# Load and store pieces of the full regions in a two-convolution kernel: 1, 4, 4, 3, 1 and 3, 3, 4, 3 tiles in place of 1, 3, 3, 3, 2, 1 and 2, 3, 3, 3, 2

## The chip, the core and the metric

One core of a Trainium2 chip runs the whole program. The metric is device microseconds of one execution; a change is read against the median of the runs before. Engines are named as the profile names them: PE (TensorE matmul), PEld (its weight loads), DVE (VectorE), ACT (ScalarE), POOL (GpSimd), SP (SyncE, which here only issues transfers). SPq and ACTq are the transfer queues of SP and ACT.

## The reference

Input x has 16 heads of 1024 x 1024 float32 (64 MB); the output has the same shape. Two layers follow each other:

```
y   = x + bias(t, s, head)            # bias: a small ReLU network of log distance, lower triangle
out = y (w + 1) + (y qw1) qw2 + (y kw1) kw2 + y qdd + y kdd
```

The first layer adds to each head a bias that depends on row t and column s only through their distance and a scale per row. The second mixes the 16 heads at every (t, s): a part of the 16 x 16 mixing matrix depends on the row t (w, qw1, qw2, qdd), a part on the column s (kw1, kw2, kdd).

## The kernel before, in words

**Tiles.** The 1024 columns are cut into 8 blocks of 128, so that 16 heads x 8 blocks fill 128 partitions. A tile is 8 rows (8 x 128 = 1024 floats a partition, 512 KB in all), and there are 128 tiles. They go in 11 regions (`REGION_TILES`, L22): region 0 has 6 tiles, regions 1 to 9 have 13 (the full ones), region 10 has 5.

**Homes.** SBUF holds three homes of 13 tile slots. Region k has home k mod 3: its x is loaded one slot further on than its y, y is written over it, and the mixed result goes to the home of region k+2. So x of region k+2 can land in a slot only when the result of region k that lies there has been stored. The last tile of x of a region lies in slot 0 of the next home, where the first result tile of the region before last lies.

**Steps.** PE takes each region in 16 column steps (`b_columns`, L763 to L774) and then one row step for each tile (`a_rows`, L750 to L761). ACT and DVE take the results of the column steps to the home in turn (L528, L641), and DVE adds those of a row step to them (`finish_tile`, L643 to L651); after that the tile can be stored. Between these steps lies the bias of the tiles of the next region: POOL makes the hidden layer (L462), ACT its ReLU (L501), PE multiplies it by the small weights (`bias_tile`, L776 to L792), and DVE (L671, L677) and ACT (L512) add the bias to x. Tile 0 of the next region has its turn at column step 4, tile 1 at step 5, then about one tile for every two steps; tile 12 comes at row step 11 (`bias_step`, L184). From tile 64 on (region 4) there are two hidden tiles for each tile in place of one.

**Row matrices.** The 16 x 16 matrices of the row steps lie in DRAM (a_mats) in chunks of 4 tiles. SP loads a chunk into one of two buffers (`load_mats_a`, L328 to L334, 4 transfers), and POOL spreads it (L439) for PE, four tiles ahead of the row step. POOL does this in line with the hidden tiles, so a chunk that comes late holds up the hidden tiles too.

**Transfers.** A load piece is 8 transfers, one for each block (`load_x`, L315 to L326), all on SP. A store piece is 8 transfers too: 4 on SP (`store_upper`, L336 to L340) and 4 on ACT, in two portions of 2 at the two row steps after the piece's last tile (`portions_at`, L282, and L542 to L547). A load waits for the stores that free its slots, by one semaphore for each store piece (`out_done`).

**The order on SP** is written out by hand (L382 to L406): for region k and its row steps T = 0 to 12, SP first issues the chunk of row matrices that falls due there (every fourth tile, so the T differs from region to region: 0, 4, 8, 12 in regions 1, 5 and 9; 3, 7, 11 in 2 and 6; 2, 6, 10 in 3 and 7; 1, 5, 9 in 4 and 8), then at T = 6 the last piece of x of region k+1, then the store piece whose last tile is T (the last store piece a step early in the list), then at T = 7, 10 and 12 (`AHEAD`) the pieces 0, 1 and 2 of x of region k+2. The pieces that are left (3 and 4) come first in the list of region k+1. Each of these waits in line: a store piece waits until DVE has finished its last tile, and all that stands behind it on SP waits with it.

In what follows S0, S1, ... are the store pieces of the region, X0, X1, ... the load pieces of region k+2, XL the last load piece of region k+1, and M with a number the chunk that falls due at that row step. The list between the first store and X2 is then, for a region 1 as an example:

```
before: M0 S0(T1) M4 S1(T4) XL(T6) S2(T7) X0(T7) M8 S3(T10) X1(T10) S4(T11) M12 X2(T12)
after:  M0 S0(T2) M4 S1(T5) XL(T6) X0(T7) M8 S2(T9) X1(T10) S3(T11) M12 X2(T12)
```

Of the kernel before, what the change touches and what calls it, by code (L numbers as in the profile page):

```python
# [21 lines left out]
REGION_TILES = (6,) + (13,) * 9 + (5,)  # L22
REGIONS = len(REGION_TILES)
# [2 lines left out]
HALF_TILES = ALL_TILES // 2  # L26
HOME_TILES = max(REGION_TILES)
HOMES = 3
STORE_PIECES = {6: (2, 2, 2), 13: (2, 3, 3, 3, 2), 5: (2, 1, 1, 1)}
STORE_SEMS = max(len(sizes) for sizes in STORE_PIECES.values())  # L30
LOAD_PIECES = {6: (1, 2, 3), 13: (1, 3, 3, 3, 2, 1), 5: (1, 4)}
AHEAD = (7, 10, 12)
PORTIONS = (2, 2)
CHUNK = 32
# [25 lines left out]
def build(nc, x, W1, b1, W2, b2, c, L_mult, init_L, qw1, qw2, kw1, kw2, qdd, kdd, w, out):  # L60
# [6 lines left out]
    with ExitStack() as ctx:  # L67
# [84 lines left out]
        def tile_of(k, T):  # L152
            return FIRST_TILE[k] + T
# [19 lines left out]
        def a_tile(k, T):  # L173
            return SETUP_TILES + FIRST_TILE[k] + COL_TILES * (k + 1) + T
# [5 lines left out]
        def emptied(i):  # L180

            return main_taken[i % 2], i // 2 + 1
# [32 lines left out]
        def piece_start(sizes, i):  # L215
            return sum(sizes[:i])

        def times(pieces, i, k):

            return sum(i < len(pieces(r)) for r in range(k + 1))  # L220

        def store_pieces(k):
            return STORE_PIECES[REGION_TILES[k]]

        def load_pieces(k):
            return LOAD_PIECES[REGION_TILES[k]]

        def piece_of(sizes, T):
            return min(i for i in range(len(sizes)) if T < sum(sizes[:i + 1]))
# [13 lines left out]
        def x_slot(k, T):  # L243
            return (y_slot(k, T) + 1) % (HOMES * HOME_TILES)
# [25 lines left out]
        def home_rows(b, slot, n):  # L270
            return of_block(homes, HOMES * HOME_TILES * COLS, b, slot * COLS, [[W, n], [1, W]])

        def store_block(eng, k, i, b):
            T, n = piece_start(store_pieces(k), i), store_pieces(k)[i] * ROWS
            t0 = tile_of(k, T) * ROWS
            return eng.dma_start(out[0, :, t0:t0 + n, b * W:(b + 1) * W], home_rows(b, mixed_slot(k, T), n))  # L276
# [29 lines left out]
        @block.sync  # L306
        def _(sp):
            def load_compact(part, v1, v2, vd):
                for dst, src in ((first[part], v1), (second[part], v2)):
                    sp.dma_start(dst.rearrange("p (b i) -> p b i", b=BLOCKS),  # L310
                                 src.rearrange("o (b p) g i m -> p (o b) (g i m)", p=P)).then_inc(weights_in[part], DMA)
                sp.dma_start(diag[part].rearrange("p (b m) -> p b m", b=BLOCKS),
                             vd.rearrange("o (b p) g m -> p (o b) (g m)", p=P)).then_inc(weights_in[part], DMA)

            def load_x(k, i):  # L315
                T, n = piece_start(load_pieces(k), i), load_pieces(k)[i]
                if k >= 1 and T + 1 >= HOME_TILES:

                    sp.wait_ge(out_done[0], times(store_pieces, 0, k - 1) * PER_PIECE)
                elif k >= 2 and T + 1 < REGION_TILES[k - 2]:  # L320
                    left = piece_of(store_pieces(k - 2), min(T + n, REGION_TILES[k - 2] - 1))
                    sp.wait_ge(out_done[left], times(store_pieces, left, k - 2) * PER_PIECE)
                t0 = tile_of(k, T) * ROWS
                for b in BLOCK_ORDER:
                    sp.dma_start(home_rows(b, x_slot(k, T), n * ROWS),
                                 x[0, :, t0:t0 + n * ROWS, b * W:(b + 1) * W]).then_inc(x_in[i], DMA)  # L326

            def load_mats_a(v):  # L328
                if v >= A_RING:
                    sp.wait_ge(unit_ready, (v - A_RING + 1) * (CHUNK // UNIT))  # L330
                for g in range(GROUPS):
                    src = bass.AP(a_mats.tensor, v * H * H * CHUNK, [[H * CHUNK, H], [0, GS], [1, H * CHUNK]])
                    sp.dma_start(mats_in[GP * g:GP * (g + 1), v % A_RING * H * CHUNK:(v % A_RING + 1) * H * CHUNK], src)\
                        .then_inc(a_in[v % A_RING], DMA)  # L334

            def store_upper(k, i):  # L336
                taken, count = emptied(a_tile(k, piece_start(store_pieces(k), i + 1) - 1))
                sp.wait_ge(taken, count)
                for b in BLOCK_ORDER[sum(PORTIONS):]:
                    store_block(sp, k, i, b).then_inc(out_done[i], DMA)  # L340

            def load_mats_b():
                for b in range(BLOCKS):
                    sp.dma_start(of_block(mats_b, RGP * W, b, (b // GS % WIDE * GP + b % GS) * W, [[GS * W, H], [1, W]]),
                                 b_mats[b]).then_inc(b_in, DMA)

            def save_mats(part):
                for half in range(2):
                    taken, count = emptied(turned_tile(part, half))
                    sp.wait_ge(taken, count)  # L350
                    src = turned[part][:, half * COLS:(half + 1) * COLS]
                    m = slice(half * (H // 2), (half + 1) * (H // 2))
                    if part == "b":
                        dst = b_mats[:, m].rearrange("b m n j -> (m n) b j")
                        src = src.rearrange("p (b j) -> p b j", b=BLOCKS)
                    else:
                        dst = a_mats[:, m].rearrange("v m n e -> (m n) v e")
                        src = src.rearrange("p (v e) -> p v e", e=CHUNK)
                    sp.dma_start(dst, src).then_inc(mats_out[part], DMA)

            load_compact("b", kw1, kw2, kdd)
            load_x(0, 0)
            load_compact("a", qw1, qw2, qdd)
            sp.dma_start(w_eye, w.rearrange("g m n -> g (m n)").partition_broadcast(P)).then_inc(weights_in["a"], DMA)
            load_x(0, 1)
            load_x(0, 2)
            save_mats("b")
            sp.wait_ge(mats_out["b"], 2 * DMA)
            sp.wait_ge(mats_zeroed, 1)
            load_mats_b()  # L370
            for i in range(3):
                load_x(1, i)
            save_mats("a")
            load_x(1, 3)
            sp.wait_ge(mats_out["a"], 2 * DMA)
            for v in range(A_RING):
                load_mats_a(v)
            load_x(1, 4)
            sp.wait_ge(tables_made, 3)
            sp.dma_start(late_scales, scale_late).then_inc(scales_out, DMA)  # L380
            loaded = [3, 5] + [0] * (REGIONS - 2)
            for k in range(REGIONS):  # L382

                while k + 1 < REGIONS and loaded[k + 1] < min(5, len(load_pieces(k + 1))):
                    load_x(k + 1, loaded[k + 1])
                    loaded[k + 1] += 1
                if k == 3:
                    sp.wait_ge(scales_out, DMA)
                    sp.wait_ge(nd_ready, PART // 2 // ROWS)
                    sp.dma_start(row_scale[:, 0:PART // 2], late_scales[:, 0:PART // 2]).then_inc(scales_in, DMA)  # L390
                if k == 5:
                    sp.wait_ge(nd_ready, PART // ROWS)
                    sp.dma_start(row_scale[:, PART // 2:], late_scales[:, PART // 2:]).then_inc(scales_in, DMA)
                for T in range(REGION_TILES[k]):
                    v = chunk_behind(tile_of(k, T))
                    if v is not None:
                        load_mats_a(v)
                    if k + 1 < REGIONS and len(load_pieces(k + 1)) > 5 and T == min(6, REGION_TILES[k] - 4):
                        load_x(k + 1, 5)
                    for i in range(len(store_pieces(k))):  # L400
                        if T == piece_start(store_pieces(k), i + 1) - 1 - (i == 4 and k < REGIONS - 1):
                            store_upper(k, i)
                    if k + 2 < REGIONS and (T in AHEAD or k == 0 and T == REGION_TILES[0] - 1) \
                            and loaded[k + 2] < len(load_pieces(k + 2)):
                        load_x(k + 2, loaded[k + 2])
                        loaded[k + 2] += 1  # L406
            for i in range(len(out_done)):
                sp.wait_ge(out_done[i], times(store_pieces, i, REGIONS - 1) * PER_PIECE)
# [429 lines left out]
```

## Time and profile before

| what | value |
|---|---|
| median of 3 runs | 895.82 us |
| lowest and highest run | 891.65 and 903.48 us |
| the profiled execution | 896.75 us |
| its span in the trace | 894.9 us |
| mean granted TensorE clock | 0.894 of full |
| PE, DVE, ACT, POOL busy | 78%, 54%, 44%, 57% of the span |
| read from and written to HBM | 77.61 MB and 69.47 MB |

The span runs from the first to the last instruction of the trace; 1.85 us of the profiled execution lie around it. A busy share is a mean over stages with different limits: in the first half of the tiles POOL has one hidden tile for each tile, in the second half two.

### The profile page before, as it was taken

How to read it: one execution, taken by the hardware profiler on the slowest of the kernel's cores; microseconds unless marked ns; L12 is line 12 of the kernel's file. 1: busy time of each engine (PE TensorE's matmuls, PEld its weight loads, DVE VectorE, ACT ScalarE, POOL GpSimd, SP SyncE). 2: the span in 40 equal slices, each digit the busy share in tenths (PEclk: the TensorE clock that was granted, in tenths of full speed). 3: DMA queues.
4: the chain of work that ended last, by engine and by line, in shares of the span. 5: the costliest groups of instructions: out<-in, count | busy, mean ns of one | idle time of the engine just before them, and what ended most of it. 6: DMA issues, size and time to landing. Idle time of an engine off the chain costs nothing. (4 is left out here: it accounts for less than half of the span.)

```text
span 894.9 us, 28881 instructions
## 1 busy us (share of the span) xinstructions
PE 699.0 (78%) x12836; PEld 586.1 (65%) x12836; DVE 481.0 (54%) x629; ACT 395.8 (44%) x428; POOL 513.4 (57%) x463
## 2 busy tenths in 40 slices
PE   0466767986998798696699859969988896699764
PEld 0254566875887688585577657756866685589664
DVE  7667625863693595475346625653475365335412
ACT  5756536544743663563245325433543453232000
POOL 4524823734475257368558937985898588635300
PEclk9876978988998899899899979998999999799857
DMA  6578559597778979877885888589859897843905
GB/s 129 137 169 147 132 145 205 128 227 169 181 185 208 208 149 223 213 159 150 189 195 125 201 185 188 113 185 215 183 123 184 180 198 151 212 111 73 258 7 118
DMA packets 302936, 148.98 MB, mean 166 GB/s; under 512 B 31964, under 2 KB 298588, under 8 KB 302812
## 3 DMA queue, kind: packets, MB, share of 16 engines
q1 hardware_dynamic: 232928, 113.56, 57.5%
q10 hardware_dynamic: 69884, 33.58, 16.3%
q8 instruction: 101, 1.65, 0.8%
q14 instruction: 23, 0.19, 0.1%
HBM read 77.61 MB, written 69.47 MB: 164 GB/s over the span
## 5 line engine op out<-in xcount | busy, mean ns | idle before, releaser
L462 POOL TENSOR_TENSOR hidden<-log_table,row_scale 128x1024 f32<-128x1024 f32 x192 | 364.3, 1913 | 218.3 <-PE bias L789 210.4
L772 PEld LDWEIGHTS main<-homes,mats_b 64*64 64x64 f32 (+1 forms) x6656 | 316.9, 189 | 150.3 <-ACT homes L528 65.1
L772 PE MATMUL main<-homes,mats_b 64*64 64x104 f32 (+2 forms) x6656 | 332.5, 274 | 106.1 <-ACT homes L528 50.7
L501 ACT ACTIVATE hidden<-hidden,b_col 128x1024 f32<-128x1024 f32 x192 | 221.0, 1152 | 259.6 <-POOL hidden L462 187.6
L759 PEld LDWEIGHTS main<-homes,mats_a 64*64 64x64 f32 x4096 | 239.2, 136 | 51.3 <-issue 37.4
L759 PE MATMUL main<-homes,mats_a 64*64 64x128 f32 x4096 | 256.0, 279 | 5.2 <-POOL mats_a L439 3.5
L439 POOL TENSOR_TENSOR mats_a<-mats_in,own_block 128x256 f32<-128x256 f32 x256 | 153.6, 655 | 143.0 <-DMA mats_in<-a_mats 112.9
L651 DVE TENSOR_TENSOR homes<-main,homes 128x1024 f32<-128x1024 f32 x128 | 156.7, 1225 | 59.4 <-PE main L759 54.3
L641 DVE COPY homes<-main 128x832 f32<-128x832 f32 (+1 forms) x80 | 77.7, 971 | 192.1 <-PE main L772 189.2
L789 PE MATMUL bias<-hidden,w_blocks 64*32 64x256 f32 (+1 forms) x2048 | 120.4, 528 | 58.0 <-ACT hidden L501 46.4
L677 DVE SCALAR_TENSOR_TENSOR homes<-bias,b_col,homes 64x256 f32<-64x256 f32 x256 | 122.9, 480 | 76.7 <-DMA homes<-in_x 52.8
L528 ACT ACTIVATE homes<-main 128x832 f32<-128x832 f32 (+2 forms) x96 | 73.4, 764 | 141.2 <-PE main L772 125.9
L671 DVE SCALAR_TENSOR_TENSOR homes<-bias,b_col,homes 128x512 f32<-128x512 f32 x128 | 90.3, 747 | 68.0 <-PE bias L789 58.2
L512 ACT ACTIVATE homes<-homes,b_col 64x512 f32<-64x512 f32 x128 | 89.9, 754 | 63.5 <-DMA homes<-in_x 52.3
L789 PEld LDWEIGHTS bias<-hidden,w_blocks 64*32 64x32 f32 x2048 | 24.8, 108 | 79.4 <-issue 60.2
L298 DVE TENSOR_TENSOR homes<-homes 128x2048 f32<-128x2048 f32 x4 | 12.3, 3123 | 0.1
L719 PE MATMUL bias<-relu_b,w_blocks 64*32 64x1 f32 x4 | 0.3, 191 | 13.7 <-DVE w_blocks L626 13.7
L719 PEld LDWEIGHTS bias<-relu_b,w_blocks 64*32 64x32 f32 x4 | 0.2, 136 | 13.6 <-issue 13.6
L495 ACT ACTIVATE mats_b<-zero_col 128x8192 f32<-128x8192 f32 x1 | 7.0, 7012 | 0.0
L712 PE MATMUL main<-homes 128*128 128x128 f32 x32 | 5.6, 350 | 0.6 <-DVE homes L606 0.6
L712 PEld LDWEIGHTS main<-homes 128*128 128x128 f32 x32 | 5.0, 183 | 1.5 <-issue 0.8
L601 DVE TENSOR_TENSOR homes<-homes 128x2048 f32<-128x2048 f32 x2 | 4.6, 2292 | 0.1
(40 smaller groups left out, 33.0 us busy)
## 6 DMA issues: line engine op xcount, KB each, us to landing
homes<-in_x SPq DMA_DIRECT2D x224, 192.0 KB, 6.2
out_mixed<-homes SPq DMA_DIRECT2D x108, 192.0 KB, 4.8
out_mixed<-homes ACTq DMA_DIRECT2D x108, 192.0 KB, 5.4
out_mixed<-homes SPq DMA_DIRECT2D x88, 128.0 KB, 3.5
out_mixed<-homes ACTq DMA_DIRECT2D x88, 128.0 KB, 3.6
homes<-in_x SPq DMA_DIRECT2D x160, 64.0 KB, 4.4
homes<-in_x SPq DMA_DIRECT2D x80, 128.0 KB, 4.5
mats_in<-a_mats SPq DMA_DIRECT2D x128, 64.0 KB
```

Of the source, the lines that this page charges most:

```text
L439: spread_half = nc.gpsimd.tensor_tensor(bass.AP(mats_a, w % A_RING_UNITS * A_UNIT + q * GP, [[A_RING_UNITS * A_UNIT, P], [GS, H], [1, GS], ...
L462: nc.gpsimd.tensor_tensor(hidden_tile(u, g).rearrange("p (j b s) -> p j b s", b=2, s=W), bass.AP(log_table, t0 - SLOTS * W * g, [[2 * TABL ...
L501: nc.scalar.activation(hidden_tile(u, g), hidden_tile(u, g), ACT.Relu, bias=b1_col[:, 0:1])\
L512: add = nc.scalar.activation(y_rows(high_half, k, T, b), x_rows(high_half, k, T, b), ACT.Identity, bias=b2_col[high_half, 1:2])
L528: nc.scalar.activation(mixed_columns(k, C), column_sums(k, C), ACT.Copy)\
L641: dve.tensor_copy(mixed_columns(k, C), column_sums(k, C)).then_inc(main_taken[b_tile(k, C) % 2], 1)
L651: dve.tensor_tensor(at, main[:, i % 2, :], at, ALU.add).then_inc(main_taken[i % 2], 1)
L671: add = dve.scalar_tensor_tensor(out=y_rows(whole, k, T, b), in0=falling(u, b), scalar=b2_col[:, 0:1], in1=x_rows(whole, k, T, b), op0=ALU ...
L677: add = dve.scalar_tensor_tensor(out=y_rows(low_half, k, T, b)[:, some], in0=falling_part(u, part, b), scalar=b2_col[low_half, 0:1], in1=x ...
L759: mm = pe.matmul(main[of_wide(g), i % 2, j * W:(j + 1) * W], a_weights(g, w, j), y_row(k, T, g, j), start=True, stop=True)
L772: mm = pe.matmul(main[at, i % 2, j * W:j * W + REGION_TILES[k] * ROWS], b_weights(at, C * ROWS + j), y_column(k, at, C * ROWS + j), start= ...
L789: mm = pe.matmul(bias[quadrant(q), u % 2, b * BANK:b * BANK + n * W], w2_blocks[of, :], rows[:, b, part * n:(part + 1) * n, :], start=True ...
```

## The change

Full regions are loaded in pieces of 1, 4, 4, 3 and 1 tiles and stored in pieces of 3, 3, 4 and 3. That is 8 load transfers and 8 store transfers (4 on SP, 4 on ACT) fewer for each of the nine full regions, with the same bytes. The four load pieces before the last are again followed by `AHEAD` and by the head of the next region's list, which now holds one piece (3) in place of two. Regions 0 and 10 keep their pieces.

```diff
--- before.py
+++ after.py
@@ -26,9 +26,9 @@
 HALF_TILES = ALL_TILES // 2
 HOME_TILES = max(REGION_TILES)
 HOMES = 3
-STORE_PIECES = {6: (2, 2, 2), 13: (2, 3, 3, 3, 2), 5: (2, 1, 1, 1)}
+STORE_PIECES = {6: (2, 2, 2), 13: (3, 3, 4, 3), 5: (2, 1, 1, 1)}
 STORE_SEMS = max(len(sizes) for sizes in STORE_PIECES.values())
-LOAD_PIECES = {6: (1, 2, 3), 13: (1, 3, 3, 3, 2, 1), 5: (1, 4)}
+LOAD_PIECES = {6: (1, 2, 3), 13: (1, 4, 4, 3, 1), 5: (1, 4)}
 AHEAD = (7, 10, 12)
 PORTIONS = (2, 2)
 CHUNK = 32
@@ -222,6 +222,10 @@
         def store_pieces(k):
             return STORE_PIECES[REGION_TILES[k]]
 
+        def loads_ahead(k):
+
+            return len(load_pieces(k)) - (REGION_TILES[k] == HOME_TILES)
+
         def load_pieces(k):
             return LOAD_PIECES[REGION_TILES[k]]
 
@@ -375,13 +379,14 @@
             sp.wait_ge(mats_out["a"], 2 * DMA)
             for v in range(A_RING):
                 load_mats_a(v)
-            load_x(1, 4)
+            for i in range(4, loads_ahead(1)):
+                load_x(1, i)
             sp.wait_ge(tables_made, 3)
             sp.dma_start(late_scales, scale_late).then_inc(scales_out, DMA)
-            loaded = [3, 5] + [0] * (REGIONS - 2)
+            loaded = [loads_ahead(0), loads_ahead(1)] + [0] * (REGIONS - 2)
             for k in range(REGIONS):
 
-                while k + 1 < REGIONS and loaded[k + 1] < min(5, len(load_pieces(k + 1))):
+                while k + 1 < REGIONS and loaded[k + 1] < loads_ahead(k + 1):
                     load_x(k + 1, loaded[k + 1])
                     loaded[k + 1] += 1
                 if k == 3:
@@ -395,13 +400,13 @@
                     v = chunk_behind(tile_of(k, T))
                     if v is not None:
                         load_mats_a(v)
-                    if k + 1 < REGIONS and len(load_pieces(k + 1)) > 5 and T == min(6, REGION_TILES[k] - 4):
-                        load_x(k + 1, 5)
+                    if k + 1 < REGIONS and REGION_TILES[k + 1] == HOME_TILES and T == min(6, REGION_TILES[k] - 4):
+                        load_x(k + 1, loads_ahead(k + 1))
                     for i in range(len(store_pieces(k))):
-                        if T == piece_start(store_pieces(k), i + 1) - 1 - (i == 4 and k < REGIONS - 1):
+                        if T == piece_start(store_pieces(k), i + 1) - 1 - (REGION_TILES[k] == HOME_TILES and i == len(store_pieces(k)) - 1 and k < REGIONS - 1):
                             store_upper(k, i)
                     if k + 2 < REGIONS and (T in AHEAD or k == 0 and T == REGION_TILES[0] - 1) \
-                            and loaded[k + 2] < len(load_pieces(k + 2)):
+                            and loaded[k + 2] < loads_ahead(k + 2):
                         load_x(k + 2, loaded[k + 2])
                         loaded[k + 2] += 1
             for i in range(len(out_done)):
```

## Rows read from the trace of the kernel before

**Rows 1.** Busy time of each engine, share of the span, instructions (the page).

```profile
PE 699.0 (78%) x12836; PEld 586.1 (65%) x12836; DVE 481.0 (54%) x629; ACT 395.8 (44%) x428; POOL 513.4 (57%) x463
```

**Rows 2.** List of waits: who waited for what, us in total, times, longest.

```profile
POOL mats_a L439 <- DMA mats_in<-a_mats: 112.9, 17, 17.6
...
DVE homes L677 <- DMA homes<-in_x: 52.8, 9, 9.7
ACT homes L512 <- DMA homes<-in_x: 52.3, 10, 12.0
```

**Rows 3.** Timeline of PE: start, us, instruction, count [idle before, releaser].

```profile
221.69 5.81 PE L772 MATMUL main<-homes,mats_b 64*64 64x104 f32 x64 [8.28 <-ACT homes L528]
...
445.92 6.72 PE L772 MATMUL main<-homes,mats_b 64*64 64x104 f32 x96 [7.95 <-ACT homes L528]
```

**Rows 4.** Timeline of SP's queue, row steps of region 1, S0 to X1.

```profile
168.09 3.41 SPq L276 DMA_DIRECT2D out_mixed<-homes  x4
171.55 3.33 SPq L333 DMA_DIRECT2D mats_in<-a_mats  x4
175.59 4.41 SPq L276 DMA_DIRECT2D out_mixed<-homes  x4
180.04 8.23 SPq L325 DMA_DIRECT2D homes<-in_x  x8
188.32 4.42 SPq L276 DMA_DIRECT2D out_mixed<-homes  x4
192.78 6.29 SPq L325 DMA_DIRECT2D homes<-in_x  x8
199.12 3.19 SPq L333 DMA_DIRECT2D mats_in<-a_mats  x4
202.35 2.69 SPq L276 DMA_DIRECT2D out_mixed<-homes  x4
205.09 9.69 SPq L325 DMA_DIRECT2D homes<-in_x  x8
```

**Rows 5.** Timeline of DVE, bias of tile 1 in region 2.

```profile
219.38 1.97 DVE L677 SCALAR_TENSOR_TENSOR homes<-bias,b_col,homes 64x256 f32<-64x256 f32 x4 [9.65 <-DMA homes<-in_x]
```

**Rows 6.** Busy time by stretch, S0 to X1's landing; last three: granted clock, DMA share, GB/s.

```profile
168.00:219.40 51.40, 41.61 (x728) 36.80 (x724) 29.64 (x44) 18.96 (x23) 29.82 (x32) 0.91 0.88 193
```

**Rows 7.** Timeline of DVE: tiles 2 to 5 of region 2, tiles 4 and 5 of region 4.

```profile
248.03 2.46 DVE L651 TENSOR_TENSOR homes<-main,homes 128x1024 f32<-128x1024 f32 x2
...
252.40 2.46 DVE L651 TENSOR_TENSOR homes<-main,homes 128x1024 f32<-128x1024 f32 x2
...
405.92 1.23 DVE L651 TENSOR_TENSOR homes<-main,homes 128x1024 f32<-128x1024 f32 x1 [0.38 <-PE main L759]
407.73 1.23 DVE L651 TENSOR_TENSOR homes<-main,homes 128x1024 f32<-128x1024 f32 x1 [0.59 <-PE main L759]
```

**Rows 8.** Timeline of SP's queue: X1 of region 7, S2 and X1 of region 8.

```profile
697.04 8.14 SPq L325 DMA_DIRECT2D homes<-in_x  x8
...
758.36 2.67 SPq L276 DMA_DIRECT2D out_mixed<-homes  x4
...
775.10 9.16 SPq L325 DMA_DIRECT2D homes<-in_x  x8
```

**Rows 9.** Timeline of SP's queue: M5 and M9 of region 4.

```profile
411.94 2.67 SPq L333 DMA_DIRECT2D mats_in<-a_mats  x4
...
432.79 3.41 SPq L333 DMA_DIRECT2D mats_in<-a_mats  x4
```

**Rows 10.** Timeline of POOL: spreading after a wait, regions 4, 6 and 9.

```profile
440.63 1.19 POOL L439 TENSOR_TENSOR mats_a<-mats_in,own_block 128x256 f32<-128x256 f32 x2 [8.48 <-DMA mats_in<-a_mats]
...
600.11 1.20 POOL L439 TENSOR_TENSOR mats_a<-mats_in,own_block 128x256 f32<-128x256 f32 x2 [3.75 <-DMA mats_in<-a_mats]
...
831.21 4.65 POOL L439 TENSOR_TENSOR mats_a<-mats_in,own_block 128x256 f32<-128x256 f32 x8 [4.14 <-DMA mats_in<-a_mats]
```

**Rows 11.** Issues by size: times, KB each, median us to landing (the page).

```profile
homes<-in_x SPq DMA_DIRECT2D x224, 192.0 KB, 6.2
...
homes<-in_x SPq DMA_DIRECT2D x8, 256.0 KB, 7.5
```

## The prediction

> **What bounds the kernel now.** I began with the busy times. PE, the busiest engine, works 78% of the span [rows 1], so some 196 us of it are gaps, and the question is who makes them. The list of waits names two late transfers: row matrices, for which POOL waited 112.9 us in 17 waits, and x, for which DVE and ACT waited 52.8 and 52.3 us, mostly side by side [rows 2]. PE's timeline shows where this is paid. Early in the column steps of nearly every region PE stands still: 8.28 us in region 2, 7.95 us in region 5 [rows 3]. The releaser is ACT each time, but ACT was itself held. In region 2, ACT and DVE waited for x of tile 1, which came at 219.38 after a wait of 9.65 us [rows 5]. In region 5, POOL had waited 8.48 us, up to 440.63, for a chunk of row matrices [rows 10], and ACT's next ReLU stood in line before the copy that PE needed.
>
> Both transfers come from SP's list, so I read SP's queue next. In region 1 it issues without a break from 175.59 to 214.78 [rows 4], while the DMA engines are 88% busy at 193 GB/s [rows 6]. The list begins when DVE finishes the first tiles and ends with X1, issued from 205.09; so PE's gap moves by exactly as much as X1, or the late M, moves against the start of the row steps. The rest of a region is PE's own work or POOL's, which the change leaves alone. So I work out for each region how far the transfer that ends its gap moves.
>
> **The change part by part.** It has four terms.
>
> a) S1 waits for tile 5 in place of tile 4. In the first half DVE finishes the pair in 2.46 us, so 1.23 us later; in the second half 407.73 - 405.92 = 1.8 us later [rows 7]. S0 also waits a tile longer (tile 2), and in regions 1 and 2 a chunk stands between S0 and S1. In region 2 tile 2 is done at 248.03 + 1.23 = 249.3; S0 and M take 3.41 + 3.33 = 6.7 us [rows 4], so S1 starts at 256.0, 2.4 us behind the end of tile 4 at 253.6. I take +2.4 in regions 1 and 2. In region 3 the chunk (T = 2) is now issued ahead of S0, which leaves +1.2. In the second half row steps come more slowly and the chunk fits between the two: +1.8.
>
> b) S2 moves from T = 7 to T = 9 and so behind X0, and behind a chunk due at T = 8 or 9. For these SP's line is shorter by one S2: 4.42 us in region 1 [rows 4], 2.67 us in region 8 [rows 8], the first and the last of eight, whose mean is 3.5: -3.5.
>
> c) Ahead of X1 there now stand S0, S1, S2 with 10 tiles, where S0 to S3 with 11 stood. One S of four tiles takes the place of an S3 of three, which took 2.69 us [rows 4]. By bytes four tiles take 4/3 of it, by issues the same: 0 to +0.9. I take +0.9, since a load of 64 KB transfers took 6.29 us and one of 192 KB 9.69 us [rows 4]: size counts.
>
> d) X1 has 4 tiles in place of 3. Region 8 shows eight 256 KB issues in 9.16 us (x of region 10 has such a piece); seven with 192 KB took 9.69 us (first) to 8.14 us (last), mean 8.1 [rows 4, 8]: +1.1. By the median landing times it is 7.5 - 6.2 = +1.3 [rows 11], by bytes alone 0.52 MB at 193 GB/s = +2.7 [rows 6]; the least is -0.5, the first against the 256 KB row. The row with the size itself is nearest.
>
> Fewer issues: 8 loads and 4 stores fewer on SP cost nothing ahead of X1 beyond (b) and (c), the rest lie behind X1, where SP catches up. ACT loses 4 issues a region, beside waits of its own: 0, at the most -2.6 us a region in ACT time, covered by its wait for PE or POOL. What is late next is X2, four tiles from tile 5, wanted eight column steps after tile 1, some 8 x 2.2 = 17.5 us (half of 252.40 - 248.03 for a step [rows 7]). It is issued behind S3 (at most 4.0) and a chunk (2.7) and takes 9.2: 15.9 us behind X1, a slack of 1.6 us. At 193 GB/s X2 alone takes 10.9 us and the slack is gone: 0 to +0.1 here, up to 2 us a region if S3 or M is slow. I take 0.
>
> XL is issued by (a) later. It ends the row steps of regions 1 and 2 with a PE gap, but X1 ends a gap behind it, so that is covered. In the second half XL needs S0's ACT half, issued two row steps later; up to +1 us in regions 4 to 8, 0 taken.
>
> **The sum.** Regions whose gap ends with X1: region 0 issues x of region 2 in a run, so (d) alone, +1.1. Regions 1 and 2: 2.4 - 3.5 + 0.9 + 1.1 = +0.9 each. Region 3: -0.3. Region 7, with 1.8 for (a): +0.3. Together +2.9.
>
> Regions whose gap ends with a chunk. In 4 and 8 the chunk at T = 5 now stands ahead of S1's wait, where it was issued at 411.94 behind it; that shortens the line to M9 by its 2.67 us [rows 9], and S2 is gone from it too (2.7 to 2.8 us in both): 1.8 - 2.7 - 2.7 = -3.6 each. The earlier wait for M5 vanishes, but POOL then only reaches M9 sooner, so its gain isn't added. Region 5 (M8): 1.8 - 3.5 = -1.7. Region 6 waits for M7, up to 600.11 [rows 10]; it stands behind S1 and XL but was ahead of S2 already: +1.8. Region 9 waits for M4, up to 831.21 [rows 10], behind S0, which opens a tile later: +1.8. Together -3.6 x 2 - 1.7 + 1.8 + 1.8 = -5.3.
>
> 2.9 - 5.3 = -2.4 us. Against the profiled execution, 896.75 us (span 894.9), that is 894.4; the median, 0.93 us lower, gives 893.4. I forecast 893.5 us: no difference that can be told, since about 2% (18 us) is what a measurement here tells from none.
>
> **The rivals.** *Faster: SP's issuing is the bound, not the bytes.* Then (c) and (d) are 0, and (a) is covered because SP is behind anyway. For it: between M4's end (174.88) and S1 (175.59) SP waited only 0.7 us, then not at all up to X1 [rows 4]. Regions 1, 2, 3, 5 and 7 gain 3.5 each, 4 and 8 2.7 + 2.7 each: -17.5 - 10.8 = -28, 868 us. Against it: the DMA share of 0.88, and the 192 KB pieces that take longer to issue than the 64 KB ones. The Trainium skill (DMA: Bandwidth & Descriptors, section Rules for kernel authors) says many small transfers should be coalesced into a large one; it speaks for this rival. The trace agrees only in part: 256 KB lands in 7.5 us against 6.2, less than by its bytes [rows 11].
>
> *Slower: the DMA engines are the bound from S0 to X1's landing.* Up to that landing 18 tiles' worth must pass: S0 to S3 (11), S4's ACT half (1), XL, X0 and X1 (5), two chunks (1). After it is S0 to S2 (10), S3's ACT half (1.5), 6 tiles of x, the chunks: 18.5. S2 behind X0 then gains X1 nothing. The half tile is 0.26 MB at 193 GB/s = 1.4 us, the later start is (a), and X1's extra tile comes last of all, with none of its transfers complete before: 2.7 by bytes. That is 2.4 + 1.4 + 2.7 = 6.5 in regions 1 and 2, 5.3 in 3, 5.9 in 7, 2.7 in 0; 6 and 9 pay 1.8 each; 4, 5 and 8 lose their gain. Sum +31, 927 us; it decides when X1 lands over 53 us behind the old S0 in region 1. Against it: 12% of that stretch is idle, 6 us, enough to take the half tile; with the extra tile at 1.1 and no half tile it is half, some 910 us. The Trainium skill (DMA: Bandwidth & Descriptors, section Issuing engines are not separate DMA queues) says that transfers of SP and ACT run on the same 16 DMA engines, which is why ACT's halves count here. The trace agrees as far as SP's issues stretch to 1 us apiece at 180.04 while ACT stores [rows 4].
>
> **How the numbers follow.** The forecast has 0.60, the faster rival 0.22, the slower 0.18. Half of the faster one's price is 882, which is still within 2%; below 877.9 (faster by over 2%) I put 0.16, above 913.7 (slower) 0.12, within 0.72. The range leaves a tenth on each side: the faster one's 870 at the one end, a little over the slower one's half price, 914, at the other. The forecast's own range, from the bounds of c, d and the 1 us of XL, is 884 to 905.
>
> **What would show it.** In SP's queue of region 1 after the change: S1 some 2 us later against the row steps, X0 and M8 about 1 us earlier, S2 directly ahead of X1, X1 some 9 to 10 us long and landing within 2 us of before (51.3 us behind the old S0). The total of POOL's waits for row matrices should fall by 5 to 15 us, with the waits for M5 in regions 4 and 8 gone and that in region 6 longer; DVE's and ACT's waits for x should stay within 10 us. I am wrong if X1 lands over 3 us earlier or later in most regions, or if DVE waits at tile 5, for X2.

## The result and the profile after

The changed kernel takes 927.34 us (median of 4 runs, 925.97 to 928.00), the kernel before 893.74 us beside it (891.29 to 903.48): a ratio of 1.0347 with an interval of 1.0295 to 1.0399. By the medians it is slower by 33.6 us; 893.5 was forecast, and the range ended at 914. The profiled execution took 927.26 us (span 925.4). Here and below a ratio leaves out executions in a slower state (one of four in run 10, two of ten in run 11), and a median does not.

The page's busy line after the change, to be read beside [rows 1]. The engines do the same work, only the span is longer, so the time came as gaps.

```profile
PE 698.4 (75%) x12836; PEld 584.7 (63%) x12836; DVE 479.6 (52%) x629; ACT 395.6 (43%) x428; POOL 513.3 (55%) x463
```

The list of waits after, for [rows 2] (line, what was waited for, us in total, times, longest). The waits for row matrices rose by 5 us, those of ACT for x from 52.3 to 78.2, those of DVE from 52.8 to 73.3. The second DVE line for x, L676, works in the second half of the tiles and had 9.8 us in two waits before. Of its five waits now, four are for tile 1: 5.64, 2.74 and 2.95 us in the column steps of regions 5, 6 and 7, where nothing was waited for before, and 12.85 us in those of region 8, where it was 8.63.

```profile
POOL mats_a L444 <- DMA mats_in<-a_mats: 118.3, 17, 16.2
ACT homes L517 <- DMA homes<-in_x: 78.2, 10, 12.3
...
DVE homes L682 <- DMA homes<-in_x: 73.3, 10, 11.8
...
DVE homes L676 <- DMA homes<-in_x: 24.8, 5, 12.8
```

PE's timeline after, at the places of [rows 3] (start, us, what, in brackets the idle time ahead and its end): the gap early in region 2's column steps is now 10.46 us, where it was 8.28. The one in region 5 fell a little, from 7.95 to 7.56 us.

```profile
236.94 5.81 PE L777 MATMUL main<-homes,mats_b 64*64 64x104 f32 x64 [10.46 <-ACT homes L533]
...
468.74 6.52 PE L777 MATMUL main<-homes,mats_b 64*64 64x104 f32 x96 [7.56 <-ACT homes L533]
```

SP's queue in region 1 after, for [rows 4]: S0, M4, S1, then XL and X0 in one row of 16 issues, M8, S2, X1.

```profile
180.56 4.39 SPq L280 DMA_DIRECT2D out_mixed<-homes  x4
184.99 4.81 SPq L337 DMA_DIRECT2D mats_in<-a_mats  x4
189.85 3.66 SPq L280 DMA_DIRECT2D out_mixed<-homes  x4
193.55 14.49 SPq L329 DMA_DIRECT2D homes<-in_x  x16
208.08 2.51 SPq L337 DMA_DIRECT2D mats_in<-a_mats  x4
210.63 6.08 SPq L280 DMA_DIRECT2D out_mixed<-homes  x4
216.75 11.11 SPq L329 DMA_DIRECT2D homes<-in_x  x8
```

DVE's timeline after, the first instruction on tile 1 and the first on tile 5, for [rows 5]: tile 1 came at 234.62, tile 5 was hardly waited for.

```profile
234.62 1.97 DVE L682 SCALAR_TENSOR_TENSOR homes<-bias,b_col,homes 64x256 f32<-64x256 f32 x4 [11.84 <-DMA homes<-in_x]
...
253.14 1.98 DVE L682 SCALAR_TENSOR_TENSOR homes<-bias,b_col,homes 64x256 f32<-64x256 f32 x4 [0.63 <-DMA homes<-in_x]
```

The stretch after that answers to [rows 6] (stretch and us, busy of PE, PEld, DVE, ACT and POOL, granted clock, DMA share, GB/s). It begins 1.6 us ahead of S0; from S0 on the DMA share is 0.85 and the rate 191 GB/s, where 0.88 and 193 stood. On average the DMA engines are not fuller than before.

```profile
179.00:234.60 55.60, 39.41 (x700) 34.53 (x694) 28.00 (x39) 18.89 (x22) 28.06 (x31) 0.89 0.83 185
```

**Measured from the start of region 1's row steps** (162.95 before, 172.28 after), in us:

| | S0 | S1 | XL | M8 | X1 issued from | to | tile 1 landed |
|---|---|---|---|---|---|---|---|
| before | 5.1 | 12.6 | 17.1 | 36.2 | 42.1 | 51.8 | 56.4 |
| after | 8.3 | 17.6 | 21.3 | 35.8 | 44.5 | 55.6 | 62.3 |

S1 opens 4.9 us later. With S2 gone from behind XL, M8 is level again. S2 at 6.08 us in place of S3's 2.69 then sets X1 back by 2.3. X1 itself adds 3.6, of which 1.4 in issuing and 2.2 between its last issue and its landing (4.6 before, 6.8 after).

The same reading for all the regions whose late issue of X1 was forecast to end a gap, in us against the kernel before (the region is that of the row steps in which X1 is issued; the landing is the last of its eight):

| region | 1 | 2 | 3 | 7 |
|---|---|---|---|---|
| forecast | +0.9 | +0.9 | -0.3 | +0.3 |
| X1 landed | +5.9 | +4.9 | +5.8 | +3.8 |
| of it: X1 begun | +2.3 | +0.4 | +2.9 | +0.8 |
| X1's eight issues | +1.4 | +4.1 | +2.3 | +2.4 |
| from its last issue to its landing | +2.2 | +0.4 | +0.6 | +0.6 |

So X1 itself costs 2.9 to 4.5 us more, 3.5 in the mean, and outside region 1 most of it lies in issuing. X1 of region 2, before and after:

```profile
283.53 6.53 SPq L325 DMA_DIRECT2D homes<-in_x  x8
```
```profile
299.27 10.63 SPq L329 DMA_DIRECT2D homes<-in_x  x8
```

**Where the time arises**, from PE's timeline: by how much the first row step or column step of a region starts later than before (the two profiled executions lie 30.5 us apart). The largest single steps are region 1's beginning, then 5.7 to 6.6 from one region's row steps to the next in regions 1 to 4, and 6.7 in the column steps of region 8. Two stretches give 4.5 back each: rows of 4 to columns of 5, and rows of 8 to columns of 9.

| region | 1 | 2 | 3 | 4 | 5 | 6 | 7 | 8 | 9 | 10 |
|---|---|---|---|---|---|---|---|---|---|---|
| column steps | +6.3 | +13.6 | +18.1 | +24.7 | +23.2 | +22.6 | +28.4 | +25.7 | +27.9 | +29.8 |
| row steps | +9.3 | +15.3 | +21.1 | +27.7 | +22.6 | +26.2 | +27.2 | +32.4 | +27.4 | +30.5 |

Set against the prediction's sum (a region's share runs from its row steps to those of the next, region 0's from region 1's column steps): 6.3 us at region 1's beginning, for which it has no term; 26.6 in regions 0, 1, 2, 3 and 7 together, put at +2.9; and -2.4 in regions 4, 5, 6, 8 and 9, put at -5.3.

The 6.3 us at region 1 come before any store of a full region. At the start SP issues three pieces of region 1's x, then writes the row matrices to DRAM (`a_mats`), issues a fourth piece, and only then loads the first chunks of row matrices. SP's queue and POOL there, before: the three pieces are seven tiles.

```profile
43.75 20.01 SPq L325 DMA_DIRECT2D homes<-in_x  x24
63.80 7.82 SPq L359 DMA_DIRECT2D a_mats<-homes  x2
...
80.51 7.81 SPq L333 DMA_DIRECT2D mats_in<-a_mats  x8
```
```profile
87.33 4.75 POOL L439 TENSOR_TENSOR mats_a<-mats_in,own_block 128x256 f32<-128x256 f32 x8 [6.96 <-DMA mats_in<-a_mats]
```

And after: the three pieces are nine tiles, 26.65 us in place of 20.01, and POOL starts on the row matrices 5.35 us later. Its hidden tiles stand behind them, and PE's second row step of region 0 begins at 102.41, where it was 97.09.

```profile
43.22 26.65 SPq L329 DMA_DIRECT2D homes<-in_x  x24
69.91 7.39 SPq L363 DMA_DIRECT2D a_mats<-homes  x2
...
86.76 6.68 SPq L337 DMA_DIRECT2D mats_in<-a_mats  x8
```
```profile
92.68 4.62 POOL L444 TENSOR_TENSOR mats_a<-mats_in,own_block 128x256 f32<-128x256 f32 x8 [8.35 <-DMA mats_in<-a_mats]
```

### The profile page after: what moved, and what is told of

Read it like the earlier page. It is cut to its first block and busy times, and to the rows that moved or that the text cites. A ratio compares the mean times of both kernels' runs of the same rounds, so it can differ in the third digit from the quotient of the medians.

```text
span 925.4 us, 28737 instructions
## 1 busy us (share of the span) xinstructions
PE 698.4 (75%) x12836; PEld 584.7 (63%) x12836; DVE 479.6 (52%) x629; ACT 395.6 (43%) x428; POOL 513.3 (55%) x463
## 5 line engine op out<-in xcount | busy, mean ns | idle before, releaser
L777 PE MATMUL main<-homes,mats_b 64*64 64x104 f32 (+2 forms) x6656 | 331.9, 274 | 123.7 <-ACT homes L533 62.2
L764 PEld LDWEIGHTS main<-homes,mats_a 64*64 64x64 f32 x4096 | 236.3, 134 | 55.8 <-issue 40.5
L764 PE MATMUL main<-homes,mats_a 64*64 64x128 f32 x4096 | 253.4, 278 | 10.3 <-POOL mats_a L444 9.4
L682 DVE SCALAR_TENSOR_TENSOR homes<-bias,b_col,homes 64x256 f32<-64x256 f32 x256 | 122.9, 480 | 100.6 <-DMA homes<-in_x 73.3
L676 DVE SCALAR_TENSOR_TENSOR homes<-bias,b_col,homes 128x512 f32<-128x512 f32 x128 | 90.3, 747 | 75.1 <-PE bias L794 50.4
L517 ACT ACTIVATE homes<-homes,b_col 64x512 f32<-64x512 f32 x128 | 89.7, 753 | 87.2 <-DMA homes<-in_x 78.2
L302 DVE TENSOR_TENSOR homes<-homes 128x2048 f32<-128x2048 f32 x4 | 12.3, 3122 | 0.1
L525 ACT ACTIVATE homes<-main 128x1024 f32<-128x1024 f32 x4 | 4.0, 1023 | 2.0 <-PE main L717 2.0
```

What stands on the lines that cost most here:

```text
L517: add = nc.scalar.activation(y_rows(high_half, k, T, b), x_rows(high_half, k, T, b), ACT.Identity, bias=b2_col[high_half, 1:2])
L676: add = dve.scalar_tensor_tensor(out=y_rows(whole, k, T, b), in0=falling(u, b), scalar=b2_col[:, 0:1], in1=x_rows(whole, k, T, b), op0=ALU ...
L682: add = dve.scalar_tensor_tensor(out=y_rows(low_half, k, T, b)[:, some], in0=falling_part(u, part, b), scalar=b2_col[low_half, 0:1], in1=x ...
L764: mm = pe.matmul(main[of_wide(g), i % 2, j * W:(j + 1) * W], a_weights(g, w, j), y_row(k, T, g, j), start=True, stop=True)
L777: mm = pe.matmul(main[at, i % 2, j * W:j * W + REGION_TILES[k] * ROWS], b_weights(at, C * ROWS + j), y_column(k, at, C * ROWS + j), start= ...
```

## The experiments

Ratios are against the kernel before, timed beside them on the same chip: 895.55 us for runs 1 to 4, 897.26 for 5 to 8, 894.58 for 9 to 12. In all of them but run 4 a load also waits for every store piece whose tiles it overwrites, not for the last one only; the changed kernel itself waits for the last one. No cost of it is seen: SP's waits for stores ahead of loads come to 5.6 us in the changed kernel, to none in run 1, and to 5.0 to 5.4 in runs 2, 3, 5, 6 and 9.

**1. The loads alone.**

```diff
-STORE_PIECES = {... 13: (3, 3, 4, 3) ...}
+STORE_PIECES = {... 13: (2, 3, 3, 3, 2) ...}
```

> The change's load pieces (1, 4, 4, 3, 1) with the old store pieces (2, 3, 3, 3, 2). Theory A (x of the first waited piece, X1, comes late because it is 4 tiles and the transfer engines are full): the gap in regions 1 to 3 grows by about 3.5 us each, the start by 6 us, x of region 2 by 3 us; some 910 to 916 us. Theory B (the later gates of the store pieces S0 and S1 are what costs): only the start and region 2 are paid, 900 to 905 us. Theory C (the four-tile store S2 ahead of X1 costs): as B.

928.26 us, ratio 1.0357 (1.0320 to 1.0395): above what any theory gave. All of the loss is there with the old stores. SP's queue of region 1 shows X1, and DVE's timeline its landing:

```profile
216.23 10.50 SPq L330 DMA_DIRECT2D homes<-in_x  x8
```
```profile
233.94 1.97 DVE L683 SCALAR_TENSOR_TENSOR homes<-bias,b_col,homes 64x256 f32<-64x256 f32 x4 [16.95 <-DMA homes<-in_x]
```

Tile 1 lands 7.2 us behind the last issue and 62.2 us behind the row steps' start (171.76 here), as late as in the changed kernel. The stores aren't needed for that.

**2. The stores alone.**

```diff
-LOAD_PIECES = {... 13: (1, 4, 4, 3, 1) ...}
+LOAD_PIECES = {... 13: (1, 3, 3, 3, 2, 1) ...}
```

> The change's store pieces (3, 3, 4, 3) with the old load pieces (1, 3, 3, 3, 2, 1). Theory A: X1 is three tiles again, so regions 1 to 3 lose 2 us each at most and some of it is given back in regions 4, 5 and 8: 893 to 902 us. Theory B: +5 us in each of regions 1 to 3 and about 2 us in 6 and 9: 908 to 915 us. Theory C: 2 to 3 us in each of regions 1 to 3: 898 to 905 us.

891.22 us, ratio 0.9937 (0.9906 to 0.9969), 4 us faster. From its X1's first issue (206.11) to tile 1 it takes 14.0 us, as before (219.38 - 205.09 = 14.3):

```profile
220.12 1.97 DVE L683 SCALAR_TENSOR_TENSOR homes<-bias,b_col,homes 64x256 f32<-64x256 f32 x4 [6.26 <-DMA homes<-in_x]
```

So the terms (a), (b), (c) and the gain at M9 together are a small gain, as forecast, and the later gates alone are not the loss. They are felt, though: X1 of region 1 begins 45.0 us behind the row steps' start, where it was 42.1.

**3. The changed kernel with region 1's x in the old pieces.**

```diff
-            return LOAD_PIECES[REGION_TILES[k]]
+            return (1, 3, 3, 3, 2, 1) if k == 1 else LOAD_PIECES[REGION_TILES[k]]
```

> The changed kernel, but x of region 1 alone is loaded in the old pieces (1, 3, 3, 3, 2, 1). In the trace of the changed kernel the first row matrices are issued 6 us later than before, behind 9 tiles of x in place of 7, and region 1 begins 6 us later. If that is a cost of its own, 921 us (6 less than the changed kernel's 927). If it is covered by a later wait, 926 to 928 us.

917.34 us, ratio 1.0213 (1.0167 to 1.0258). Lower than both values: the start, of which the prediction says nothing, is worth about 10 us, and some 22 are left.

**4. The kernel before with S0 and S1 held back by a tile.**

```diff
+        def held(k, i):
+            return int(REGION_TILES[k] == HOME_TILES and i < 2)
...
-                taken, count = emptied(a_tile(k, piece_start(store_pieces(k), i + 1) - 1))
+                taken, count = emptied(a_tile(k, piece_start(store_pieces(k), i + 1) - 1 + held(k, i)))
```

(The place in SP's list and ACT's portions move with it.)

> The kernel before with all its pieces, but the store pieces S0 and S1 of full regions are issued one tile later, on both queues. Theory B: X1 moves with S1, 4 to 5 us in each of regions 1 to 3, 2 us in 6, 7 and 9, less 3 us in 4 and 8: 903 to 910 us. Theory A and C: the line to X1 catches up by its own slack, under 2 us in each of regions 1 to 3: 892 to 900 us.

906.87 us, ratio 1.0109 (1.0063 to 1.0154). Term (a) is real, and about 10 us by itself; run 2 shows that the rest of the new store layout pays for it. In region 1, S1 begins 15.0 us behind the row steps' start, 2.4 later than before, which is the price that (a) has there.

**5. X1 of three tiles again, X2 of four.**

```diff
-LOAD_PIECES = {... 13: (1, 4, 4, 3, 1) ...}
+LOAD_PIECES = {... 13: (1, 3, 4, 4, 1) ...}
```

> The change's store pieces, and five load pieces as in the change, but of 1, 3, 4, 4 and 1 tiles: X1 has three tiles again, X2 and X3 have four. Theory A (X1's own size delays tile 1 of the next region): regions 1 to 3 go back to what the run with the store pieces alone has, the start keeps half of its loss (8 tiles ahead of the first row matrices, where 9 or 7 stood): 893 to 900 us. Theory D (fewer and larger pieces cost wherever they stand): 910 us or more.

909.78 us, ratio 1.0174 (1.0114 to 1.0234): 10 us above theory A's range and at the edge of D's, so neither is met. One tile less in X1 wins 1.7 points back, although the bytes of a region are the same. What stays is the start (region 1's column steps begin 6.3 us late here too) and X2, whose four tiles now begin at tile 4 and are waited for; in the column steps of region 3:

```profile
325.02 1.97 DVE L683 SCALAR_TENSOR_TENSOR homes<-bias,b_col,homes 64x256 f32<-64x256 f32 x4 [7.45 <-DMA homes<-in_x]
```

**6. X1's four tiles as 2 and 2, issued in a run.** Bytes, places and the start stay as in the changed kernel; only the first two tiles now have transfers and a semaphore of their own. (The start-up list is written so that the same nine tiles go first.)

```diff
-LOAD_PIECES = {... 13: (1, 4, 4, 3, 1) ...}
+LOAD_PIECES = {... 13: (1, 2, 2, 4, 3, 1) ...}
...
-                        load_x(k + 2, loaded[k + 2])
-                        loaded[k + 2] += 1
+                        for more in range(2 if T == 10 and REGION_TILES[k + 2] == HOME_TILES else 1):
+                            load_x(k + 2, loaded[k + 2])
+                            loaded[k + 2] += 1
```

> The changed kernel with X1's four tiles as two pieces of two, issued one right behind the other at the same place (1, 2, 2, 4, 3, 1); the same tiles of region 1 as in the changed kernel go ahead of the first row matrices. Bytes and order of all transfers stay, only tiles 1 and 2 are signalled when their half has landed. If what costs is that tile 1 waits for the whole piece, the gap shrinks by 4 to 6 us in regions 0 to 3 and 7: 902 to 912 us. If what costs are the bytes ahead of X1, nothing is gained: 922 to 930 us.

913.64 us, ratio 1.0179 (1.0122 to 1.0237), nearer to the side of the wait for a whole piece. SP's queue, and DVE on tile 1 and on tile 5:

```profile
209.33 13.61 SPq L330 DMA_DIRECT2D homes<-in_x  x16
```
```profile
222.00 1.97 DVE L682 SCALAR_TENSOR_TENSOR homes<-bias,b_col,homes 64x256 f32<-64x256 f32 x4 [4.79 <-DMA homes<-in_x]
...
249.01 1.97 DVE L682 SCALAR_TENSOR_TENSOR homes<-bias,b_col,homes 64x256 f32<-64x256 f32 x4 [10.18 <-DMA homes<-in_x]
```

All four tiles are issued from 209.33 to 222.94, longer than in the changed kernel, and yet tile 1 is taken 12.7 us behind the first issue (17.9 there). The other half lands 17.4 us behind the first issue, nearly as late as the whole piece does (17.9). The wait then passes to the four tiles behind, the changed kernel's X2: 10.18 us at tile 5, where the changed kernel showed 0.63.

**7. X1 ahead of S2.**

```diff
-AHEAD = (7, 10, 12)
+AHEAD = (7, 8, 12)
```

> The changed kernel with X1 issued at row step 8 in place of 10, ahead of the four-tile store S2. Theory C (S2 ahead of X1 costs): regions 1 to 3 gain S2's issue, 4 to 6 us each, and region 7 some: 905 to 915 us. If ACT's half of S2 and the transfer engines hold X1 back all the same: 920 to 928 us.

955.77 us, ratio 1.0682 (1.0635 to 1.0729): no theory had this. X1 does land sooner in region 1 (57.1 us behind the row steps' start, 62.3 in the changed kernel). But where a chunk falls due at T = 9 or 10, it now stands behind X1. In regions 3, 4, 7 and 8 POOL waits 18.1 to 23.1 us for it. SP's queue in region 7 (XL, X0 and X1 in one row, S2, M10), and POOL's wait for M10:

```profile
708.10 27.40 SPq L330 DMA_DIRECT2D homes<-in_x  x24
735.55 7.97 SPq L280 DMA_DIRECT2D out_mixed<-homes  x4
743.57 2.73 SPq L338 DMA_DIRECT2D mats_in<-a_mats  x4
```
```profile
749.77 1.19 POOL L445 TENSOR_TENSOR mats_a<-mats_in,own_block 128x256 f32<-128x256 f32 x2 [23.07 <-DMA mats_in<-a_mats]
```

POOL's waits for row matrices come to 155.7 us. The run tells nothing of X1's length; it shows what a chunk pays that stands behind a long piece.

**8. A short first piece, all of it short.** Pieces of 1, 2, 3, 3, 3 and 1, X1 (two tiles) and X2 issued together at T = 10 as in run 6; this also puts six tiles in place of nine ahead of the writing of the row matrices.

```diff
-LOAD_PIECES = {... 13: (1, 4, 4, 3, 1) ...}
+LOAD_PIECES = {... 13: (1, 2, 3, 3, 3, 1) ...}
```

> The change's store pieces with loads of 1, 2, 3, 3, 3 and 1 tiles, X1 and X2 issued one behind the other at row step 10; 6 tiles of region 1 ahead of the first row matrices. Theory A carried on: X1 lands 2 to 3 us sooner than with three tiles, the start gains 3 us: 878 to 888 us. If the wait only passes on to tile 3 (X2): 888 to 895 us, as with the store pieces alone.

886.77 us, ratio 0.9895 (0.9855 to 0.9934): faster than both kernels, than the one before by about 1%.

**9. The changed kernel with the old start, X1 and X2 as 2 and 2 each.** Region 1's pieces as in run 3; the rest:

```diff
-LOAD_PIECES = {... 13: (1, 4, 4, 3, 1) ...}
+LOAD_PIECES = {... 13: (1, 2, 2, 2, 2, 3, 1) ...}
...
+                        for more in range(2 if T in (10, 12) and REGION_TILES[k + 2] == HOME_TILES else 1):
```

> The changed kernel with x of region 1 in the old pieces and, in the later full regions, the two pieces of four tiles each cut into two of two, issued one right behind the other (1, 2, 2, 2, 2, 3, 1): bytes, order and places of the changed kernel, with finer signals and 16 more issues a region. If the loss is the start and the wait of a tile for the rest of its piece, all of it is gone: 886 to 896 us, as with the store pieces alone (891). If fewer issues or the bytes matter too: over 900 us.

883.98 us, ratio 0.9856 (0.9797 to 0.9914), better than expected. Against run 3, which has the same tiles in the same places of SP's list, only the halves are new, and the ratio falls from 1.0213 to 0.9856. SP's queue and DVE in region 1:

```profile
201.04 11.90 SPq L330 DMA_DIRECT2D homes<-in_x  x16
```
```profile
211.89 1.97 DVE L684 SCALAR_TENSOR_TENSOR homes<-bias,b_col,homes 64x256 f32<-64x256 f32 x4 [5.18 <-DMA homes<-in_x]
```

The four tiles take 11.90 us to issue (11.11 in one piece), but tile 1 is there 10.9 us behind the first issue, ahead of the end of the last. The second half lands at 15.9 us.

**10. Run 8's loads with the old stores.**

```diff
-STORE_PIECES = {... 13: (3, 3, 4, 3) ...}
+STORE_PIECES = {... 13: (2, 3, 3, 3, 2) ...}
```

> The loads of 1, 2, 3, 3, 3 and 1 tiles that gave 887 us, with the old store pieces (2, 3, 3, 3, 2). If the new store pieces are worth what they gave alone (0.6%): 889 to 895 us. If the later gates of S0 and S1 cost what they cost alone (1.1%): 876 to 884 us.

884.82 us, ratio 0.9853 (0.9767 to 0.9938). Beside run 8's 0.9895 (0.9855 to 0.9934) the two store layouts can't be told apart with such loads.

**11. The kernel before with region 1's x alone in the new pieces.**

```diff
-            return LOAD_PIECES[REGION_TILES[k]]
+            return (1, 4, 4, 3, 1) if k == 1 else LOAD_PIECES[REGION_TILES[k]]
```

> The kernel before, with x of region 1 alone in the change's pieces (1, 4, 4, 3, 1), 9 tiles in place of 7 ahead of the first row matrices. If the start is a cost of its own: 6 to 10 us over the kernel before, 901 to 907 us. If region 0 hides it: under 2 us more.

903.54 us, ratio 1.0088 (1.0043 to 1.0132): some 8 us by the ratio, from the start alone. Its SP queue shows 25.53 us for the nine tiles, and region 1's column steps begin 6.4 us late.

```profile
43.18 25.53 SPq L330 DMA_DIRECT2D homes<-in_x  x24
...
85.79 6.77 SPq L338 DMA_DIRECT2D mats_in<-a_mats  x8
```

**12. Run 8 with three tiles ahead of the writing of the row matrices and nine behind their load.**

```diff
-            for i in range(3):
+            for i in range(2):
                 load_x(1, i)
...
-            load_x(1, 3)
...
-            for i in range(4, loads_ahead(1)):
+            for i in range(2, loads_ahead(1)):
                 load_x(1, i)
```

> The run with loads of 1, 2, 3, 3, 3 and 1 tiles and the new store pieces (887 us), with 3 tiles of x of region 1 in place of 6 ahead of the first row matrices and the other 9 behind them. If those bytes set the start: 3 to 6 us less, 881 to 884 us. If x of region 1 then comes late itself: 887 us or more.

893.55 us, ratio 0.9980 (0.9950 to 1.0010), behind run 8's 0.9895. The x of region 1 is now what is late: DVE waited 15.30 us for it up to 83.15. Fewer tiles ahead of the row matrices help only until x itself is wanted.

```profile
83.15 1.97 DVE L683 SCALAR_TENSOR_TENSOR homes<-bias,b_col,homes 64x256 f32<-64x256 f32 x4 [15.30 <-DMA homes<-in_x]
```

## Why the prediction was wrong

**Term (d) was undersized by a factor of three.** It was put at +1.1, from how long the pieces take to issue, and measured +2.9 to +4.5 in the four regions where X1 was forecast to end a gap. What PE's gap waits for is the landing of tile 1, and tile 1 waits for all eight transfers of its piece. From the first issue of X1 to DVE's first instruction on tile 1, in region 1:

| X1 | kernel | us |
|---|---|---|
| 3 tiles | before, run 2 | 14.3, 14.0 |
| 4 tiles in one piece | after, run 1 | 17.9, 17.7 |
| 4 tiles as 2 and 2 | run 6, run 9 | 12.7, 10.9 |

The fourth tile costs 3.6 us here. The prediction had two rows for it, 1.1 by issue and 1.3 by landing, and treated them as two estimates of one cost. They add, and the first was too small: over the four regions the eight issues of X1 took 7.9 us in the mean before and 10.5 after, and the tail behind the last issue 5.3 and 6.3. The 9.16 us that stood for eight 256 KB issues was one row of region 8; the changed kernel's took 9.7 to 11.1. Even the bound by bytes, 2.7, was too low.

The wait is for the piece and not for the tile's own bytes: in runs 6 and 9 the same four tiles, issued in the same place, let tile 1 go 5 to 7 us sooner, while all four land 17.4 and 15.9 us behind the first issue.

**The start was left out of the sum.** What the prediction says of region 0, that (d) alone counts there, looks at region 2's x. The list ahead of the row steps issues three pieces of region 1's x before the row matrices are written and loaded, and they grew by two tiles: 6.6 us more on SP, 6.3 later at region 1, and some 8 to 12 us in the end by the ratios (runs 11 and 3). The change's diff doesn't touch those lines; a piece's size does.

**The terms for the stores came near as a sum over all regions, but not ahead of X1.** Run 2 is the forecast without (d), which is -2.4 - 5 x 1.1 = -7.9 us; it measured -4.3. In region 1, (a) was +2.4 and measured 4.9; (b), -3.5, measured -4.6 (XL to M8 took 19.1 us, then 14.5); (c), 0.9, was 3.4 less 0.7 from a shorter M8. Together they were to be -0.2, and X1 began 2.3 us later. The step that failed is in (a): it priced the S0 of three tiles and the chunk behind it by their old rows, 3.41 + 3.33 us, and they took 4.39 + 4.81. In run 4, where S0 keeps two tiles, S1 moves by the 2.4 that were forecast.

**The regions whose gap ends with a chunk.** Regions 4 and 8 gained 5.1 and 5.0 us from row steps to row steps, for 3.6. Region 6's +1.8 came as +2.2 and region 9's as +2.4, both up to the next column steps. Region 5 is a miss: put at -1.7, it came out at +3.6. DVE now also waits there for tile 1 (2.74 us); how much of the 3.6 that makes is not shown.

**The signs that were named.** X1 landed 57.2 us behind the old S0, not within 2 us of 51.3. POOL's waits for row matrices rose where a fall of 5 to 15 was forecast, although those for M5 in regions 4 and 8 went, as forecast. X2 was hardly waited for (0.63 us at most), as forecast, but with X1 late itself: runs 5 and 6, where X1 comes sooner, show its wait.

**The rivals.** The faster one fell: fewer issues bought nothing, and run 9, with 16 issues more in a region than run 3 and nothing else new, takes 0.9856 where run 3 took 1.0213. The slower one named 927 us, and its deciding point was passed. For regions 0, 1, 2, 3 and 7 its prices come to 26.9 us, and 26.6 were measured. But it let regions 4 and 8 lose their gain, which they kept, and it had no start; these two nearly cancel, so that its total is met is chance in part. Its reason, that the DMA engines are the bound, is neither shown nor refuted. Their share did not rise (0.85 from S0 on, 0.88 before), yet in region 1 the four tiles of X1 need 15.9 to 17.9 us, in one piece or in halves, and no run tells whether the engines or the queue set that time.

**What the pages say.** The Trainium skill (DMA: Bandwidth & Descriptors, section Rules for kernel authors), cited ahead for coalescing many small transfers, would have favoured the changed kernel if it held for pieces of this size; here run 9, with more and smaller transfers, takes 0.9856 of the kernel before and the changed kernel 1.0347. The same page (section Anatomy of one DMA — SWDGE (gpsimd) path) says that a semaphore fires only when the transfer's last byte has landed; these transfers are issued by SP, but the table on X1 above agrees in kind. On top of that this kernel lets a tile wait for the count of all eight transfers of its piece.

**What is not told apart.** With the old stores (run 1) X1 also began 2.3 us later against the row steps, S1, S2 and X0 each taking 0.5 to 1.1 us longer than before; why was not tried. So the loss ahead of X1 can't be put down to the stores alone. Nor was it shown region by region how 6.3 us at region 1 become some 8 to 12 at the end.

## What to carry to other kernels

Size a load piece by its first consumer: the first tile waits for the whole piece, so the piece that ends a gap should be small; two halves issued in a run cost 0.8 to 3.1 us more of issuing here than one whole piece, and gave the first tile 5 to 7 us sooner. When a piece size is a shared constant, go through every list that issues a piece, the start-up too, and price what stands behind it there. A queue slot is worth what waits behind it: one piece moved ahead of a store and, in four regions, a chunk cost 28 us against the changed kernel (run 7).

## What the runs showed that was not expected

In region 1 sixteen issues of 128 KB took 11.9 and 13.6 us in runs 9 and 6, eight of 256 KB with the same bytes 10.5 and 11.1 in run 1 and after: twice the instructions cost 0.8 to 3.1 us of issuing. Where the cost of a larger transfer shows differs from place to place: in region 1 the tail behind the last issue grew from 4.6 us at 192 KB to 6.8 at 256 KB, in regions 2, 3 and 7 by no more than 0.6 us, and the issuing grew by 2.3 to 4.1 us instead. The medians from issue to landing rose from 6.2 us before to 7.8. The DMA issues of the page after (KB each, median us to landing):

```profile
homes<-in_x SPq DMA_DIRECT2D x152, 256.0 KB, 7.8
...
homes<-in_x SPq DMA_DIRECT2D x80, 192.0 KB, 6.0
```
